# State-space stage: the convolution folded into the projection, as four shifted products into 48 rows per batch

## The reference, cut to what matters

```python
h = _layernorm(x) * (1 + ca) + sa                     # per batch, [512, 128]
xc = depthwise_conv(h, conv_w, pad=1) + conv_b        # 4 taps per channel, 511 outputs
xc = pad(xc, to=512)                                  # the last position is zero
proj = xc @ Win + b_in                                # 128 -> 16 + 32 + 32
delta = proj[..., :16]
B_in = proj[..., 16:48].reshape(.., 16, 2).mean(-1)
C    = proj[..., 48:80].reshape(.., 16, 2).mean(-1)
A = -exp(A_log);  dA = softplus(delta) * A;  A_bar = exp(dA)
B_bar = where(|A| < eps, 1 + dA/2 + dA*dA/6, (A_bar - 1) / A) * B_in
h_t = A_bar_t * h_(t-1) + B_bar_t                     # scan over 512 positions
x = x + ga * (C * h @ Wout + b_out)
```

## Time and profile before

| | |
|---|---|
| median of 3 runs | 1054.12 us (1053.44 to 1055.52) |
| the profiled execution's own time | 1047.75 us |
| its span in the profile | 1045.9 us |
| mean granted clock of PE | 0.895 |
| busy share: PE, DVE, ACT, POOL | 80%, 71%, 60%, 49% |
| chain that ended last: PE, DVE, POOL, issue, ACT | 47%, 17%, 13%, 10%, 8% |
| line L1726 (the taps) in that chain | 2% |

### The profile page before, as it was taken

One profiled execution on the slowest core, in us unless ns is written; L12 is line 12 of the kernel. 1 busy time (PEld: TensorE's weight loads), 2 busy tenths in 40 slices (PEclk: granted clock), 3 DMA queues, 4 the chain that ended last, 5 costly groups with the idle time before them and its releaser, 6 DMA issues.

```text
span 1045.9 us, 14141 instructions
## 1 busy us (share of the span) xinstructions
PE 841.4 (80%) x4604; PEld 461.2 (44%) x4604; DVE 738.1 (71%) x1572; ACT 630.5 (60%) x1098; POOL 515.6 (49%) x816
## 2 busy tenths in 40 slices
PE   4669999999999886878787999999625558876995
PEld 3312222222222221212266877777424437765873
DVE  5588888888888874745257777778559875855672
ACT  1237877777787664747466777777425525454662
POOL 3344372727272645436183057776679236543121
PEclk9669999999999997959699999999866868989997
DMA  6474645455554460302113266666150000000000
GB/s 201 85 192 123 145 139 129 144 123 153 115 170 97 136 150 34 132 25 95 36 51 116 74 231 238 236 233 233 62 219 1 0 0 1 1 11 11 11 21 30
DMA packets 44308, 109.98 MB, mean 105 GB/s; under 512 B 7422, under 2 KB 20222, under 8 KB 38726
## 3 DMA queue, kind: packets, MB, share of 16 engines
q1 hardware_dynamic: 38172, 96.75, 31.3%
q0 software_dynamic: 4992, 10.36, 2.9%
q10 hardware_dynamic: 1072, 1.98, 0.7%
HBM read 57.65 MB, written 51.03 MB: 104 GB/s over the span
## 4 chain that ended last, share of the span: by engine, by line
PE 47%; DVE 17%; POOL 13%; issue 10%; ACT 8%; DMA 2%; another core or an unknown queue 2%; ACTq 0%; POOLq 0%; DVEq 0%
PE PS L1031 12%; PE PS L1020 8%; POOL yd L1222 7%; PE PS L1004 5%; DVE mx L857 4%; PE PS L318 2%; PE PS L320 2%; DVE cb L2141 2%; PE PS L319 2%; ACT E L778 2%; PE PS L986 2%; DVE XC L1726 2%; PE PS L975 2%; ACT ov L784 1%
## 5 line engine op out<-in xcount | busy, mean ns | idle before, releaser
L857 DVE TENSOR_REDUCE mx<-PS 128x2 f32<-128x1024 f32 x256 | 306.1, 1221 | 103.8 <-PE PS L1004 82.0
L778 ACT ACTIVATE E<-PS 128x512 f32<-128x512 f32 x512 | 277.0, 600 | 105.2 <-PE PS L1020 84.6
L1020 PE MATMUL PS<-Q,K 51*128 51x512 bf16 x512 | 169.2, 404 | 22.6 <-issue 18.2
L1031 PE MATMUL PS<-E,V 128*9 128x512 f32 x1024 | 144.9, 641 | 19.4 <-ACT ov L784 18.2
L1004 PE MATMUL PS<-K,Q 48*128 48x512 bf16 x512 | 142.5, 413 | 21.5 <-DVE mx L857 19.5
L1020 PEld LDWEIGHTS PS<-Q,K 51*128 51x128 bf16 x512 | 37.0, 95 | 180.8 <-ACT E L778 90.3
L1222 POOL DMA_INDIRECT yd<-yt,goes x92 | 96.6, 1050 | 38.9 <-issue 23.2
L1376 DVE TENSOR_TENSOR Gl<-Gf,Gh 128x512 fp32r<-128x512 f32 x116 | 81.4, 703 | 30.9 <-ACT Gh L1257 28.5
L509 POOL DMA_INDIRECT xs<-HT,pos x64 | 62.8, 981 | 45.6 <-issue 29.3
L1251 ACT ACTIVATE Gf<-PS,WR 128x512 f32<-128x512 f32 x92 | 63.3, 688 | 35.4 <-PE PS L320 28.0
L655 POOL CAST mh<-mx 128x32 bf16<-128x32 f32 x16 | 3.4, 210 | 145.3 <-DVE mx L857 145.3
(11 more groups left out here) (400 smaller groups left out, 1900.7 us busy)
## 6 DMA issues: line engine op xcount, KB each, us to landing
WR<-wsd SPq DMA_DIRECT2D x23, 1028.0 KB
xs<-zero SPq DMA_DIRECT2D x8, 2112.0 KB, 8.0
wsd<-wsp SPq DMA_DIRECT2D x8, 1024.0 KB, 4.1
Q<-dqk SPq DMA_DIRECT2D x16, 384.0 KB, 5.7
HT<-xs SPq DMA_DIRECT2D x23, 264.0 KB
dqk<-SPL SPq DMA_DIRECT2D x30, 192.0 KB, 2.8
K<-dqk SPq DMA_DIRECT2D x15, 384.0 KB, 8.7
stage<-in_w SPq DMA_DIRECT2D x9, 516.0 KB
```

The lines of the kernel that those rows point to most:

```text
L778: e.activation(E[:, m % 4, n % 4], PS[:, bank["exp", n], :], ACT.Exp).then_inc(*k.inc("exp", n))
L857: e.tensor_reduce(mx[:, 2 * s % 96:2 * s % 96 + 2], PS[:, o:o + 2, :], AX.X, ALU.max, negate=True).then_inc(*k.inc("max", s))
L1020: e.matmul(PS[:, o, :], K[r, b % 3, h // 2, kt * P:(kt + 1) * P], Q[r, b % 3, h // 2, :], start=True, stop=True).then_inc(*k.inc("exp_mm", n))
L1031: p = e.matmul(PS[32 * j:32 * j + 9, PVB, :], V[:, b % 3, kt, 4 * g + j, :], E[:, m % 4, j, :], start=(kt == 0), stop=(kt == 3))
```

## The change

The convolution is linear and works on each channel alone, so tap j can be folded into the projection's weights: `WJ[:, j] = WP * taps[:, j]`, four tables of 48 columns. The projection of a batch becomes four products with the activations shifted by j positions, 4 times 3 matmuls, into 48 partitions of a PSUM bank of its own (two banks in turn). ACT copies the 48 rows to SBUF with the convolution's bias taken through the weights (`cbs`, one small matmul), into `pj`; SP moves 16 rows at a time, three transfers per batch, to partitions 16b to 16b+15 of `TP`, which the scan reads in place of PSUM. The first tap on ACT, the three taps on DVE, `XC` and its halves go; the halves are now of `Hc`, 515 wide.

```diff
@@ ffn0, DVE: state_weights
-                    k.wait_ge("const", "wp0")
-                    e.tensor_copy(WP[:, 0, 112:128], Win[:, 0:16]).then_inc(*k.inc("v"))
...
-                    for i in range(3):
-                        k.wait_own("v")
-                        e.tensor_copy(WPh[:, i], WP[:, i]).then_inc(*k.inc("v"))
-                        k.wait_own("v")
-                        e.tensor_tensor(WPl[:, i], WP[:, i], WPh[:, i].bitcast(F32), ALU.subtract).then_inc(*k.inc("wpl", i))
+                    e.tensor_copy(WP[:, 0:16], Win[:, 0:16])
...
+                    for j in range(4):
+                        m = e.tensor_scalar(WJ[:, j], WP[:], taps[:, j:j + 1], None, ALU.mult)
...
+                    e.tensor_copy(WPh[:], WJ[:]).then_inc(*k.inc("v"))
+                    k.wait_own("v")
+                    e.tensor_tensor(WPl[:], WJ[:], WPh[:].bitcast(F32), ALU.subtract).then_inc(*k.inc("wpl"))
@@ ffn0, POOL
-                e.memset(WP[:], 0.0).then_inc(*k.inc("const", "wp0"))
@@ ssm, SP
+                for b in range(NB):
+                    k.wait_ge("pj", b)
+                    for i in range(3):
+                        e.dma_start(TP[16 * b:16 * b + 16, i], pj[16 * i:16 * i + 16, b % 2]).then_inc(*k.dma(f"tp{b % 2}", b))
@@ ssm, POOL
-                e.memset(Hc[:, :, 513:516], 0.0)
-                e.memset(XC[:], 0.0).then_inc(*k.inc("const", "hc0"))
+                e.memset(pj[:, :, 511:512], 0.0)
+                e.memset(Hc[:, :, 513:515], 0.0).then_inc(*k.inc("const", "hc0"))
@@ ssm, ACT: conv, xch
-                    if b >= 5:
-                        k.wait_ge("taps", b - 5)
-                    e.activation(Hc[:, b % 5, 1:513], PS[:, 5 + b % 3, :], ACT.Identity, bias=mf[:, 1, 0, b:b + 1],
+                    if b >= 3:
+                        k.wait_ge("xl", "s", b - 3)
+                    e.activation(Hc[:, b % 3, 1:513], PS[:, 5 + b % 3, :], ACT.Identity, bias=mf[:, 1, 0, b:b + 1],
                                  scale=mf[:, 1, 1, b:b + 1]).then_inc(*k.inc("hT", "s", b))
                     k.wait_ge("hT", "s", b)
                     if b >= 3:
-                        k.wait_ge("xl", "s", b - 3)
-                    e.activation(XC[:, b % 3, 0:511], Hc[:, b % 5, 0:511], ACT.Identity, bias=W["convb"],
-                                 scale=cw[:, 0:1]).then_inc(*k.inc("xc", "s", b))
-
-                def xch(b):
-                    k.wait_ge("taps", b)
-                    if b >= 3:
                         k.wait_ge("proj_mm", b - 3)
-                    e.activation(XCh[:, b % 3], XC[:, b % 3], ACT.Copy).then_inc(*k.inc("xh", "s", b))
+                    e.activation(Hch[:, b % 3], Hc[:, b % 3], ACT.Copy).then_inc(*k.inc("xh", "s", b))
+
+                def projected(b):
+                    k.wait_ge("proj_mm", b)
+                    if b >= 2:
+                        k.wait_ge(f"tp{b % 2}", b - 2)
+                    e.activation(pj[:, b % 2, 0:511], PS[0:48, b % 2, 0:511], ACT.Identity, bias=cbs[:]).then_inc(
+                        *k.inc("pj", b))
@@ ssm, ACT: the loop
+                k.wait_ge("cb_mm")
+                e.activation(cbs[:], PS[0:48, 2, 0:1], ACT.Copy).then_inc(*k.inc("cbs"))
+                k.wait_ge("cbs")
                 for b in range(NB + 3):
                     if 1 <= b <= NB:
                         z(b - 1)
                     if 2 <= b < NB + 2:
                         conv(b - 2)
                     if b >= 3:
-                        xch(b - 3)
+                        projected(b - 3)
@@ ssm, DVE: the loop and the scan
-                    if 2 <= b < NB + 2:
-                        taps(b - 2)
-                    if b >= 3:
-                        low(b - 3)
+                    if 2 <= b < NB + 2:
+                        low(b - 2)
...
-                k.wait_ge("proj_mm", NB - 1)
-                e.tensor_scalar(T(0), PS[:, 0, :], b5[:, 0:1], None, ALU.add).then_inc(*k.inc("v"))
+                k.wait_ge("tp0", NB - 2)
+                k.wait_ge("tp1", NB - 1)
+                e.tensor_scalar(T(0), TP[:, 0], b5[:, 0:1], None, ALU.add).then_inc(*k.inc("v"))
@@ ssm, PE
-                    c = slice(112 - 16 * b, 240 - 16 * b)
                     k.wait_ge("xl", "s", b)
-                    for i in range(3):
-                        m = product(e, PS[:, i, :], (WPh[:, i, c], WPl[:, i, c]), (XCh[:, b % 3], XCl[:, b % 3]),
-                                    b == 0, b == NB - 1)
+                    if b >= 2:
+                        k.wait_ge("pj", b - 2)
+                    for j in range(4):
+                        m = product(e, PS[0:48, b % 2, :], (WPh[:, j], WPl[:, j]),
+                                    (Hch[:, b % 3, j:j + 512], Hcl[:, b % 3, j:j + 512]), j == 0, j == 3)
                     m.then_inc(*k.inc("proj_mm", b))
...
+                e.matmul(PS[0:48, 2, 0:1], WP[:], W["convb"], start=True, stop=True).then_inc(*k.inc("cb_mm"))
```

More of the change, by code:

```diff
@@ L158, in adaln_kernel @@
         cv = sb("cv", [P, 12])
-        WPl = sb("WPl", [P, 3, 240], F32R)
+        WP = sb("WP", [P, 48])
+        WPl = sb("WPl", [P, 4, 48], F32R)
         GBr = GC
-        WPh = sb("WPh", [P, 3, 240], F32R)
+        WPh = sb("WPh", [P, 4, 48], F32R)
         R = ExitStack()
@@ L1156, in ffn0 @@
             Gl = sb("Gl", [P, 8, 512], F32R, B)
-            WP = sb("WP", [P, 3, 240], F32, B)
+            WJ = sb("WJ", [P, 4, 48], F32, B)
             B.close()
@@ L1161, in ffn0 @@
             xt = HT[:].rearrange("p (s t) d -> p s t d", t=4)
-            Win, b5 = (stage[:].rearrange("p a n -> p (a n)")[:, o:o + n] for o, n in ((PACK2_AT["Win"], 80), (PACK2_AT["bin5"], 5)))
+            Win, b5, taps = (stage[:].rearrange("p a n -> p (a n)")[:, PACK2_AT[x]:PACK2_AT[x] + n]
+                             for x, n in (("Win", 80), ("bin5", 5), ("convw", 4)))
             bank = {}
@@ L1584, in ssm @@
             Zs = sb("Zs", [P, 4, 4, P], F32, C)
[L1585 to L1588, removed]
+            Hc = sb("Hc", [P, 3, 515], F32, C)
+            Hch = sb("Hch", [P, 3, 515], F32R, C)
+            Hcl = sb("Hcl", [P, 3, 515], F32R, C)
+            pj = sb("pj", [48, 2, 512], F32, C)
+            TP = sb("TP", [P, 3, 512], F32, C)
+            Th = sb("Th", [P, 512], F32R, C)
+            Tl = sb("Tl", [P, 512], F32R, C)
+            cbs = sb("cbs", [48, 1], F32, C)
             tb = sb("tb", [P, 12, 512], F32, C)
@@ L1592, in ssm @@
             pair = lambda i: tb[:, i:i + 2].rearrange("p a n -> p (a n)")
-            b5, cw = W["bin5"], W["convw"]
+            b5 = W["bin5"]
             WO = W["WoutBD"].rearrange("p (b n) -> p b n", b=8)
@@ L1718, in act @@
                 k.wait_ge("scan")
-                e.activation(XCh[:, 0], T(10), ACT.Copy).then_inc(*k.inc("ch"))
+                e.activation(Th[:], T(10), ACT.Copy).then_inc(*k.inc("ch"))
             def dve(e, k):
-                def taps(b):
-                    o = XC[:, b % 3, 0:511]
-                    k.wait_ge("xc", "s", b)
-                    for j in range(1, 4):
-                        m = e.scalar_tensor_tensor(o, Hc[:, b % 5, j:j + 511], cw[:, j:j + 1], o, ALU.mult, ALU.add)
-                        m.then_inc(*(k.inc("v") if j < 3 else k.inc("taps", b)))
-                        if j < 3:
-                            k.wait_own("v")
                 def low(b):
@@ L1734, in low @@
                         k.wait_ge("proj_mm", b - 3)
-                    e.tensor_tensor(XCl[:, b % 3], XC[:, b % 3], XCh[:, b % 3].bitcast(F32),
+                    e.tensor_tensor(Hcl[:, b % 3], Hc[:, b % 3], Hch[:, b % 3].bitcast(F32),
                                     ALU.subtract).then_inc(*k.inc("xl", "s", b))
@@ L1798, in dve @@
                 k.wait_own("v")
-                e.scalar_tensor_tensor(T(8), PS[:, 1, :], cv[:, 0:1], T(1), ALU.add, ALU.mult).then_inc(*k.inc("v"))
+                e.scalar_tensor_tensor(T(8), TP[:, 1], cv[:, 0:1], T(1), ALU.add, ALU.mult).then_inc(*k.inc("v"))
                 k.wait_own("v")
@@ L1802, in dve @@
                 k.wait_own("v")
-                e.scalar_tensor_tensor(T(10), PS[:, 2, :], cv[:, 1:2], T(9), ALU.add, ALU.mult).then_inc(*k.inc("scan"))
+                e.scalar_tensor_tensor(T(10), TP[:, 2], cv[:, 1:2], T(9), ALU.add, ALU.mult).then_inc(*k.inc("scan"))
                 k.wait_ge("ch")
-                e.tensor_tensor(XCl[:, 0], T(10), XCh[:, 0].bitcast(F32), ALU.subtract).then_inc(*k.inc("clow"))
+                e.tensor_tensor(Tl[:], T(10), Th[:].bitcast(F32), ALU.subtract).then_inc(*k.inc("clow"))
                 for j, (hf, t) in enumerate(YJ):
@@ L1857, in pe @@
                         k.wait_ge("ch")
-                    e.matmul(o, XCh[:, 0, t * P:(t + 1) * P], WOGh[:, c, :], start=False, stop=False)
-                    e.matmul(o, XCh[:, 0, t * P:(t + 1) * P], WOGl[:, c, :], start=False, stop=False)
+                    e.matmul(o, Th[:, t * P:(t + 1) * P], WOGh[:, c, :], start=False, stop=False)
```

(3 more changed lines are left out.)

11 lines of the change are left out of this document (7 added, 4 removed).

## The result

Over 20 runs each, interleaved on one chip, the changed kernel took 1064.37 us at the median (1056.13 to 1071.35) and the kernel before 1053.48 (1049.11 to 1059.13). The ratio is **1.0103, with a 95% interval of 1.0081 to 1.0125**: 10.9 us slower. The forecast was 1067.1 in a range of 1058 to 1076.

What follows compares the result with a forecast made beforehand. VectorE, busy 6.76 of 7.00 us per batch, was taken to bound the state-space stage. Terms -1.4 + 9.9 + 4.8 - 0.3 = +13.0 on the median 1054.12 gave 1067.1 us, range 1058 to 1076.

Steps and rivals of the forecast that it cites:

- the ring: State-space loop: transposes, projection, `pj`, next-stage weights and normalising ops form one closed lap without overlap, 6.8 us before weights.
- the 6.5: State-space loop: the prediction is wrong if transposes come under 6.5 us apart; it expected 6.8 to 8.2.
- Five laps: From the transposes of batch 2 to those of 7: 38.7 us instead of 28.8, +9.9.
- TensorE, 4 transposes and 12 products: 5.0: TensorE's part of each lap, 5.0 us, taking a half-speed start to each burst.
- rival 1: State-space stage: the same ring with the clock held up, TensorE's part 3.4 us: +5.0, 1059.1 us; chance 0.18.
- The weights, 4.7: Next-stage weights on ScalarE, in four of the five laps between transposes of batches 2 and 7, add 4.7 us.
- The tail, +4.8: From the transposes of batch 7 to the scan's first op: 16.2 us instead of 11.4, including 3.7 for three transfers.
- Start -1.4: Start of the state-space stage: transposes of batch 2 begin 1.4 us earlier, as POOL's ops run without taps beside them.
- Scan -0.3: The scan's first op reads `TP` in SBUF, not PSUM, and falls from 0.76 to 0.49 us: -0.3.
- Rival 2: State-space stage: the same ring at half clock throughout: +23.0, 1077.1 us; chance 0.10.
- Rival 3: Projection: 48-column products cost half as much as 128, the ring drops under POOL's lap: -2.4, 1051.7 us; chance 0.04.
- Rival 4: No measurable change: ring at full clock, but ScalarE's 5.89 us idle ahead of `GC` disappears: +1.9, 1056.0 us; chance 0.06.

Runs made afterwards that it cites:

- the same swap: TensorE takes the projection of batch b before the transposes of batch b+2: ratio 0.9963 in the changed kernel, 1.0218 in the kernel before.
- the three-tap kernel: The changed kernel with the fourth tap left out of the computation, nine products per batch instead of twelve: ratio 1.0075 to the kernel before.

## Why the prediction was right, and where it was off

- **Direction and mechanism: right.** The waits named ahead are there: no taps, `Hcl` released by `Hch`, `pj` by TensorE, transposes by ScalarE's `Zs` in four of the five laps, a transfer ahead of the first `tb` op. Undoing the ring without removing any work brought the whole loss back and more.
- **The sizes named ahead: in part.** Laps were to be 6.8 to 8.2 apart and are 6.0 to 8.0; three lie below 6.8, and one, 6.02, below the 6.5 that I named as a sign of being wrong. It is a lap of the ring all the same, at a granted 0.99: the threshold couldn't tell a missing ring from a full clock. The way to the scan is 15.2 instead of about 16, VectorE's wait 2.5 instead of about 3.
- **Five laps, +9.9 forecast, +5.9 measured.** The mis-sized term is "TensorE, 4 transposes and 12 products: 5.0", taken for every lap. TensorE was busy 5.2, 3.4, 5.1, 4.8 and 3.4 in them: 21.96 in the sum row instead of 25.0, which is 3.0 of the 4.0. For the rest: in the lap without weights TensorE idled 1.54 instead of 1.81, since `pj` took 0.68 instead of 0.78 and copies start 0.1 before the row above them ends, which over five laps is 1.35; the lap that waited for POOL gives 0.5 of it back. My forecast and rival 1 each had one clock for all laps; it changes from lap to lap.
- **The weights, 4.7: right as a place and nearly as a size.** Moving them gave 5.0 to 5.6 up to the scan. In the change's four laps with weights TensorE idled 5.1 more than at 1.54 each, and 0.5 of that is POOL's: 4.6.
- **The tail, +4.8 forecast, +3.8 measured.** From the end of `pj(7)` to the scan's first op it took 3.3, not 3.7: a transfer landed in 2.0, not 2.5. The Trainium skill (DMA: Bandwidth & Descriptors, "Anatomy of one DMA") puts the constant part alone at about 2.0, for transfers that GpSimd issues; these are issued by SyncE, and their landing of 1.8 to 2.1 agrees. The sum by that page, 3.3, was nearer than mine. The other 0.6 lies before: `pj(7)` ended 11.9 after the transposes, not 12.5. TensorE's first burst there was 4.95 against 5.0.
- **Start -1.4: measured -1.5. Scan -0.3: measured +0.1** to the stage's end; 0.27 was gained up to the first output product and lost behind it.
- **Rival 1** (the clock held up, +5.0) did not come true, but in the stage it was no further off than the forecast: the measured 8.3 lies between its 5.0 and 13.0, 3.3 from the one and 4.7 from the other. By the time, 10.9, the forecast is nearer.
- **Rival 2** (half clock throughout) fell: two laps of five ran at full clock. **Rival 3** (a narrow product is cheap) fell: 48 columns start 0.23 or 0.43 apart, as 128 do (0.23 by the earlier trace rows, 0.43 earlier in the same stage of the kernel before). **Rival 4** fell: ScalarE still idled 4.59 ahead of `GC` and POOL 2.37 behind it, against 5.89 and 3.38, and the difference to before was clear.
- **The sum was luckier than its terms.** The stage grew by 8.3, the time by 10.9, the forecast by 13.0 on a median 0.6 above the one measured beside the change. Its error is 2.7 us; in the stage it is 4.7. That the time grew by 2.6 more than the profiled stage is not explained, and it fell on the forecast's side: to that extent the closeness is luck.
- **What the prediction missed** is a second chain, by way of POOL's `Zs`, nearly as long as the ring, which sets the lap of 6.6. It had VectorE and POOL at 6.0 a lap.

## What to carry to other kernels

Before folding work into another engine, write down for each new operation what it waits for and what stands behind it in its engine's list; if that closes a loop, count how many batches one turn spans. Here a turn of about 7 us was hidden when it spanned two batches and set the pace when it spanned one, whatever the busy shares said, and the cure was an order, not less work. When a change removes the stage that an order was made for, try the order anew: the same swap cost 25 us in the kernel before and gained 15 in the changed one.

## What the runs showed of the hardware that I had not expected

**The clock can fall inside a burst and be full at the start of one.** After 3.18 idle this burst of the changed kernel began fast and went slow with its second product (starts 0.31, 0.38, then 0.43 apart):

```profile
809.76 0.63 PE L1828 MATMUL PS<-p,Zs 128*128 128x128 f32 x4 [3.18 <-ACT Zs L314]
810.14 0.47 PE L319 MATMUL PS<-Hch,WPh 128*48 128x512 f32 x1
810.45 0.59 PE L320 MATMUL PS<-Hch,WPl 128*48 128x512 f32 x1
810.83 0.63 PE L321 MATMUL PS<-Hcl,WPh 128*48 128x512 f32 x1
811.26 0.63 PE L319 MATMUL PS<-Hch,WPh 128*48 128x512 f32 x1
```

The burst at 825.11, after 2.60 idle, stayed at full clock; the one at 831.13, after 2.59 idle, began at half. So in this stretch the idle time just before doesn't tell the level. And less work is not shorter work: with three taps the third lap had three products fewer and TensorE was busy longer, 5.15 against 5.08, at the lower clock.

**VectorE and POOL hold each other up even on tiny operands**: in the rows of the three-tap kernel the factor of the mean (`dve_ln_nm`, L306), an op of 128x4, began at 760.53 beside POOL's multiplication and ended at 761.76, with POOL's at 761.75; alone it takes 0.16. By the Trainium skill (SBUF — State Buffer, "Who interferes with whom") a VectorE op with two SBUF inputs contends with a POOL op that reads SBUF, over a shared pair of ports that is an exclusive lock. That L306 ended only when POOL's op did agrees with it.
